# A second down-projection unit moved behind the up unit and the x transposes in the third chunk of each row group

## The chip, the cores and the metric

The kernel runs on one core of one Trainium2 chip. The metric is the device time in microseconds (us); lower is better. Three runs of the kernel before gave a median of 609.52 us (609.05 to 611.1).

The core has a matrix engine (TensorE, PE in the rows), a vector engine (VectorE, DVE), an activation engine (ScalarE, ACT), a general engine (GpSimd, POOL) and a queue that starts transfers (SyncE, SP). Each works through its own list of instructions in order, and they meet at semaphores only.

## The reference, cut to what matters

A feed-forward layer with octonion weights stands beside an autocorrelation term. `x` is 2048 rows of 1024.

```python
xn = layernorm(x)                                  # over the last axis
gate = oct_ternary_linear(xn, w_gate)              # (2048, 2732)
up   = oct_ternary_linear(xn, w_up)                # (2048, 2732)
h    = silu(gate) * up
out  = x + autocorrelation(xn) + oct_ternary_linear(h, w_down)

# oct_ternary_linear: weights rounded to scale * {-1, 0, 1}, then
#   M = einsum('jik,jod->koid', S_OCT, Wq);  einsum('...id,koid->...ko', xp, M)
# autocorrelation(xn): irfft(|rfft(xn)|^2), softmax over the 6 largest lags,
#   the sum of the row rolled by these lags
```

For rows like these lag 0 outweighs all others, so the autocorrelation term is the row itself. The kernel proves this for each row by a bound (a short spectrum and a dot product of the row's two halves) and has a slow path in case it fails.

## The kernel before, in words

**Tiling.** The 2048 rows are 8 groups g of 256. The 2732 hidden values are 3 chunks of 8 x 114. The octonion product is not made by 64 small products: half of it goes through sums and differences of the weights and of the inputs (the spectral part), the other half through single terms. Every result is made of a spectral part in PSUM, eight additions by VectorE over it, and a second series of matmuls on top (the terms).

**Units.** The work is a list of units, `units`. Each takes one of four pairs of PSUM banks in turn, so a unit waits for the last reader of the unit four places ahead of it (`owner`, `take_banks`, `bank_free`). Below, the two digits are chunk and half of the outputs:

- G00 to G21: gate units, 16 matmuls spectral and 16 of terms. Their result goes through silu on ScalarE (`silu`), which frees the banks.
- U00 to U21: up units, of the same size. VectorE multiplies the result by the silu (`product`, in the rows hx by hx and acc), which frees the banks.
- N0 and N1: down units of the group before, one for each 128 rows, 96 matmuls spectral and 96 of terms. VectorE scales them and adds the residual (zx in the rows), which frees the banks.
- X0 and X1: 8 transposes each, of the even and the odd parts of the next group's normalised x. ScalarE and VectorE split them in a high and a low fp16 part and do the same with their sums (`x_high`, `x_low`, `x_sums_high`, `x_sums_low`).
- F: four matmuls of the spectrum for the bound, with four more two places later (`lags`).

At list place n, TensorE issues the spectral part of unit n and then the terms of unit n-2. VectorE does at place n `first_adds` (four, after ScalarE has copied half of the banks by `odd_two`), a due `product` (two places behind its up unit), a due output or `least`, and `second_adds` (four). X units also have `x_low` ahead and the rounding of their sums behind. A product goes to GpSimd, which makes its sums and low parts in six operations; ScalarE makes the high parts (`h_high`, and `h_sums_high` for the sums). At which place ScalarE does these two is set by the tables `high_at` and `round_at`.

**The row statistics.** Two `row_sum` fall at F and at the next G00, two `row_var` one and two places later, the reciprocal root on GpSimd, then two `normalise` on ScalarE and two `dot` on VectorE at N0, for the group whose X units follow.

**Transfers.** The SyncE queue stores the finished rows, reloads zx with the next residual rows, and loads x three groups ahead (`load_x`). All are in one list in order.

## Time and profile before

| | us |
|---|---|
| median of 3 runs | 609.52 (609.05 to 611.1) |
| profiled execution | 609.28 |
| its span, first to last instruction | 607.5 |
| one group in the regular part (start of F to start of F) | 67.33 |
| TensorE busy | 580.5 (96% of the span) |
| VectorE busy | 507.7 (84%) |

The regular part consists of the groups 2 to 6. Group 0 and the weights take the first 90 us, group 7 and the rest the time from 510.55 us on. In a row of the timeline the first number is the start from the span's beginning and the second the duration, both in us; then engine, line, operation, output and inputs, shapes and count. Square brackets at the end name the idle time of that engine just ahead and what ended it. The recorded end of one instruction may lie past the start of the next on the same engine, since they are pipelined: a series of 16 matmuls shows as 1.91 us, and the next starts 1.75 us after its start. A row of a window has its limits and length, then the busy us (and the number of instructions) of PE, PEld, DVE, ACT and POOL, the granted TensorE clock as a share of 2.4 GHz, the share of the DMA engines and GB/s.

### The profile page before, as it was taken

How to read it: one execution, taken by the hardware profiler on the slowest of the kernel's cores; microseconds unless marked ns; L12 is line 12 of the kernel's file. 1: busy time of each engine (PE TensorE's matmuls, PEld its weight loads, DVE VectorE, ACT ScalarE, POOL GpSimd, SP SyncE). 2: the span in 40 equal slices, each digit the busy share in tenths (PEclk: the TensorE clock that was granted, in tenths of full speed). 3: DMA queues.
4: the chain of work that ended last, by engine and by line, in shares of the span. 5: the costliest groups of instructions: out<-in, count | busy, mean ns of one | idle time of the engine just before them, and what ended most of it. 6: DMA issues, size and time to landing. Idle time of an engine off the chain costs nothing.

```text
span 607.5 us, 16365 instructions
## 1 busy us (share of the span) xinstructions
PE 580.5 (96%) x6728; PEld 539.8 (89%) x6728; DVE 507.7 (84%) x1229; ACT 355.4 (59%) x497; POOL 463.0 (76%) x362
## 2 busy tenths in 40 slices
PE   4898999979999999999999999999999999999996
PEld 4898998869989998899989998899989998998896
DVE  3885897969899989989888989989898989967854
ACT  4777867664557646765466545774476545543540
POOL 2404839998769977999769977999779977987920
PEclk9999999998999999999999999999999999999999
DMA  6720012001040012102040013002040112002021
GB/s 163 200 71 1 1 29 113 3 1 70 3 139 1 3 71 87 54 1 71 2 140 2 25 48 136 4 3 71 2 140 1 38 36 71 2 2 71 1 71 72
DMA packets 10235, 30.67 MB, mean 50 GB/s; under 512 B 912, under 2 KB 4016, under 8 KB 10160
## 3 DMA queue, kind: packets, MB, share of 16 engines
q1 hardware_dynamic: 9200, 28.22, 13.8%
q10 hardware_dynamic: 960, 1.40, 1.1%
q8 instruction: 53, 0.87, 0.6%
q14 instruction: 22, 0.18, 0.1%
HBM read 21.23 MB, written 8.39 MB: 49 GB/s over the span
## 4 chain that ended last, share of the span: by engine, by line
POOL 53%; issue 30%; PE 12%; DMA 2%; DVE 1%; ACT 0%; ACTq 0%; POOLq 0%
POOL hop L1320 15%; POOL hs L1314 10%; POOL hs L1315 10%; POOL hs L1310 9%; POOL hs L1309 6%; PE acc L470 5%; PE acc L395 4%; DMA hop<-in_w_gate 2%; PE acc L375 1%; PE acc L447 1%; POOL r L1268 1%; POOL hop L1317 1%; PE acc L404 0%; PE acc L368 0%; ACTq L570 0%
## 5 line engine op out<-in xcount | busy, mean ns | idle before, releaser
L470 PE MATMUL acc<-wd,hop 114*128 114x128 f16 (+1 forms) x2944 | 171.4, 220 | 1.0 <-POOL hop L1320 0.7
L470 PEld LDWEIGHTS acc<-wd,hop 114*128 114x128 f16 (+1 forms) x2944 | 168.3, 98 | 2.2 <-POOL hop L1320 0.9
L679 ACT ACTIVATE pk<-acc 114x512 f32<-114x512 f32 (+1 forms) x120 | 70.8, 590 | 71.7 <-PE acc L470 34.0
L1309 POOL TENSOR_TENSOR hs<-hx 114x512 f32<-114x512 f32 x47 | 60.2, 1282 | 68.3 <-DVE hx L1075 60.3
L1320 POOL TENSOR_TENSOR hop<-hs,hop 114x1024 f16<-114x1024 f32 x46 | 98.2, 2135 | 7.9 <-ACT hop L734 7.9
L1317 POOL TENSOR_TENSOR hop<-hx,hop 114x1024 f16<-114x1024 f32 x46 | 98.3, 2137 | 0.7 <-ACT hop L723 0.7
L375 PE MATMUL acc<-xop,wg 128*128 128x256 f16 x704 | 84.1, 273 | 4.5 <-DVE acc L1026 4.3
L723 ACT ACTIVATE hop<-hx 114x1024 f16<-114x1024 f32 x46 | 48.6, 1057 | 65.4 <-DVE hx L1075 65.4
L368 PE MATMUL acc<-xop,wg 128*128 128x256 f16 x704 | 84.2, 273 | 1.0 <-DVE hx L1075 0.9
L375 PE MATMUL acc<-xop,wu 128*128 128x256 f16 x704 | 84.1, 273 | 0.7
L368 PE MATMUL acc<-xop,wu 128*128 128x256 f16 x704 | 84.1, 273 | 0.7 <-DVE hx L1075 0.7
L978 DVE TENSOR_TENSOR bd<-acc,pk 114x256 f32<-114x256 f32 (+1 forms) x104 | 43.7, 420 | 48.2 <-ACT pk L679 48.1
L375 PEld LDWEIGHTS acc<-xop,wg 128*128 128x128 f16 x704 | 68.3, 98 | 14.2 <-DVE acc L1026 6.0
L368 PEld LDWEIGHTS acc<-xop,wu 128*128 128x128 f16 x704 | 68.7, 98 | 9.1 <-DVE hx L1075 1.0
L368 PEld LDWEIGHTS acc<-xop,wg 128*128 128x128 f16 x704 | 67.7, 98 | 10.2 <-DVE hx L1075 2.6
L375 PEld LDWEIGHTS acc<-xop,wu 128*128 128x128 f16 x704 | 67.8, 98 | 9.9 <-DVE acc L1026 2.4
L734 ACT ACTIVATE hop<-hs 114x1024 f16<-114x1024 f32 x46 | 48.6, 1057 | 45.6 <-POOL hs L1315 45.6
L1314 POOL TENSOR_TENSOR hs<-hs 114x512 f32<-114x512 f32 x47 | 62.4, 1328 | 3.7
L1315 POOL TENSOR_TENSOR hs<-hs 114x512 f32<-114x512 f32 x47 | 62.5, 1331 | 0.0
L1075 DVE SCALAR_TENSOR_TENSOR hx<-hx,few,acc 114x1024 f32<-114x1024 f32 x47 | 59.7, 1271 | 2.1 <-PE acc L395 2.1
L1310 POOL TENSOR_TENSOR hs<-hx 114x512 f32<-114x512 f32 x47 | 60.3, 1282 | 0.0
L982 DVE TENSOR_TENSOR acc<-acc,pk 114x256 f32<-114x256 f32 (+1 forms) x104 | 43.9, 422 | 0.0
(163 smaller groups left out, 922.2 us busy)
## 6 DMA issues: line engine op xcount, KB each, us to landing
xr<-in_x SPq DMA_DIRECT2D x16, 512.0 KB, 5.0
zx<-in_x SPq DMA_DIRECT2D x16, 512.0 KB, 3.9
out_y<-zx SPq DMA_DIRECT2D x16, 512.0 KB, 2.9
hop<-in_w_down SPq DMA_DIRECT2D x1, 1364.0 KB, 6.3
hop<-in_w_gate ACTq DMA_DIRECT2D x1, 1152.0 KB
hop<-in_w_up SPq DMA_DIRECT2D x1, 1152.0 KB
hop<-in_w_gate ACTq DMA_DIRECT2D x1, 192.0 KB
hop<-in_w_up SPq DMA_DIRECT2D x1, 192.0 KB
```

Source lines behind the costliest of these rows:

```text
L368: last = nc.tensor.matmul(acc[:, bank[n], s // 2, T * (s % 2):T * (s % 2 + 1)], wm[:, c, slot, :], xop[:, g % 2, form, level, :], start=s ...
L375: last = nc.tensor.matmul(acc[:, bank[n], s // 2, T * (s % 2):T * (s % 2 + 1)], wm[:, c, slot, :], xop[:, g % 2, form, level, :], start=Fa ...
L470: last = nc.tensor.matmul(acc[:, bank[n], s // 2, at:at + P], operand(g, c, t, form, level), wd[0:WIDE[c], slot, c, :], start=which == 0 a ...
L679: nc.scalar.activation(pk[0:rows, q % 2, :, :], pair[:, :, T:2 * T], ACT.Copy, scale=XS if u[0] == "X" else 1.0).then_inc(copied, 1)
L723: nc.scalar.activation(half_of(g, c, 4 * Y, 0), by_tile(h), ACT.Copy).then_inc(hhi_done, 1)
L1075: nc.vector.scalar_tensor_tensor(hx[0:CH, m % 4, :, :], hx[0:CH, m % 4, :, :], scale[0:CH, :], bank_pair(place[u], CH).rearrange("p b (i t ...
L1309: nc.gpsimd.tensor_tensor(hs[:, 4:8:2, :], h[:, 0:4:2, :], h[:, 1:4:2, :], ALU.add)
L1310: nc.gpsimd.tensor_tensor(hs[:, 5:8:2, :], h[:, 0:4:2, :], h[:, 1:4:2, :], ALU.subtract).then_inc(hpair_done, 1)
L1314: nc.gpsimd.tensor_tensor(hs[:, 0:2, :], hs[:, 4:6, :], hs[:, 6:8, :], ALU.add).then_inc(hs_done, 1)
L1315: nc.gpsimd.tensor_tensor(hs[:, 2:4, :], hs[:, 4:6, :], hs[:, 6:8, :], ALU.subtract).then_inc(hs_done, 1)
L1317: nc.gpsimd.tensor_tensor(half_of(g, c, 4 * Y, 1), by_tile(h), half_of(g, c, 4 * Y, 0), ALU.subtract).then_inc(h_free, 1)
L1320: nc.gpsimd.tensor_tensor(half_of(g, c, NJ + 4 * Y, 1), by_tile(hs[:, 0:4, :]), half_of(g, c, NJ + 4 * Y, 0), ALU.subtract).then_inc(h_rea ...
```

## The change

In groups 1 to 6 the third chunk's list G20, N1, U20, X1, G21, U21 becomes G20, U20, X1, N1, G21, U21. Group 7 has no N1 in that place and stays as it is. With it:

- `round_at` and `high_at` move the roundings of h: behind its unit, U20's high part comes five places later instead of three, U11's high part four instead of three, U10's sums six instead of five.
- The sums of X1 are rounded at the start of the next place (N1's) rather than at its end; VectorE's `x_sums_low` then stands ahead of N1's first additions.
- `normalise` comes after N0's copy on ScalarE, `dot` at the end of N0's place on VectorE; both stood ahead before.
- At the place of U21 the second additions come ahead of N1's output.
- The load of x comes ahead of the second store of a group in SyncE's list, except for the first such load.
- The halves of hop are given out in the order of writing.

Diff:

```diff
--- before.py
+++ after.py
@@ -74,11 +74,13 @@
     for g in range(1, G):
         for c in range(NC):
             units += [("G", g, c, 0)]
-            if c == 1 or c == 2 and g < G - 1:
-                units += [("N", g - 1, c - 1)]
+            if c == 1:
+                units += [("N", g - 1, 0)]
             units += [("U", g, c, 0)]
             if c and g < G - 1:
                 units += [("X", g + 1, c - 1)]
+            if c == 2 and g < G - 1:
+                units += [("N", g - 1, 1)]
             units += [("G", g, c, 1), ("U", g, c, 1)]
             if c == 2 and g < G - 1:
                 units += [("F", g + 1)]
@@ -112,7 +114,11 @@
 
     halves, free_after = {}, {(G - 1, NC - 1): [("U", G - 2, NC - 1, 1)]}
     spare = [(i, None) for i in range(8)]
-    for u in units:
+
+    def written(u):
+        return place[u] + (2.5 if u[0] == "U" and u[2:] == (2, 0) else 0)
+
+    for u in sorted((u for u in units if u[0] in "UN"), key=written):
         if u[0] == "U" and u[3] == 0 and u[1:3] != (G - 1, NC - 1):
             two = sorted(spare[:2])
             spare = spare[2:]
@@ -146,10 +152,12 @@
     for u in u_no:
         _, g, c, Y = u
         if place[u] >= OPEN:
-            late = 6 if g == 0 or c == 2 else 4 if (c, Y, g) == (1, 0, G - 1) else 5
+            inner = 1 <= g < G - 1
+            late = 6 if g == 0 or c == 2 or inner and (c, Y) == (1, 0) else 4 if (c, Y, g) == (1, 0, G - 1) else 5
             if (g, c) == (G - 1, NC - 1):
                 late = 4 + 3 * (1 - Y)
-            high_at[place[u] + 3] = u
+
+            high_at[place[u] + (5 if inner and (c, Y) == (2, 0) else 4 if inner and (c, Y) == (1, 1) else 3)] = u
             round_at[place[u] + late] = u
     for _, g, t in n_no:
         z_at[place["N", g, t] + (t if g == G - 1 else 1 if t == 0 else 2 if g == G - 2 else 3)] = (g, t)
@@ -310,10 +318,12 @@
             for g in range(G):
                 for t in range(NT):
                     k = NT * g + t
+                    if t == 1 and 0 < g and g + 3 < G:
+                        load_x(g + 3)
                     sp.wait_ge(out_done, k + 1)
                     sp.dma_start(out_rows[k, :, :], zx[:, t, :]).then_inc(out_st, 16)
-                    if t == 1 and g + 3 < G:
-                        load_x(g + 3)
+                    if t == 1 and g == 0:
+                        load_x(3)
                     if g < G - 1:
                         sp.wait_ge(out_st, 16 * (k + 1))
                         sp.dma_start(zx[:, t, :], x_rows[k + NT, :, :]).then_inc(zx_in[t], 16)
@@ -797,9 +807,6 @@
             h_high(("U", 0, 1, 0))
 
             for n in range(OPEN, N + 8):
-                if n in norm_at:
-                    normalise(norm_at[n], 0)
-                    normalise(norm_at[n], 1)
                 if n in z_at:
                     g, t = z_at[n]
                     k = NT * g + t
@@ -814,15 +821,20 @@
                     for b in range(2):
                         act.wait_ge(tail_mult, b + 1)
                         nc.scalar.activation(hx[0:CH, LAST % 4, 2 * b + 1, :], last_h[:, 2 * b + 1, :], ACT.Copy).then_inc(tail_odd, 1)
+                if n in x_sums and x_sums[n][2] == 1:
+                    x_sums_high(x_sums[n])
                 if n < N:
                     u = units[n]
                     if u[0] in "GUNX":
                         odd_two(u)
+                    if n in norm_at:
+                        normalise(norm_at[n], 0)
+                        normalise(norm_at[n], 1)
                     if u[0] == "X":
                         x_high(u)
                     if u[0] == "F":
                         power(u)
-                if n in x_sums:
+                if n in x_sums and x_sums[n][2] == 0:
                     x_sums_high(x_sums[n])
                 if n in silu_at:
                     silu(silu_at[n])
@@ -1141,9 +1153,8 @@
                 kind = u[0]
                 if kind == "X":
                     x_low(u)
-                if n in norm_at and kind == "N":
-                    dot(norm_at[n], 0)
-                    dot(norm_at[n], 1)
+                if n in x_sums and x_sums[n][2] == 1:
+                    x_sums_low(x_sums[n])
                 if u in quad_no:
                     first_adds(n, u)
                 if kind == "X":
@@ -1156,25 +1167,31 @@
                         dve.wait_ge(term_mm, prod_no[v] + 1)
                         dve.wait_ge(silu_done, LAST + 1)
                         split_last(v)
-                if n >= OPEN + 2:
-                    v = units[n - 2]
-                    if v[0] == "N":
-                        _, g, t = v
-                        pair = bank_pair(n - 2).rearrange("p b e -> p (b e)")
-                        res = zx[:, t, :]
-                        most = D - DB
-                        dve.wait_ge(term_mm, prod_no[v] + 1)
-                        dve.wait_ge(z_done, n_no[v] + 1)
-                        nc.vector.scalar_tensor_tensor(res[:, 0:most], pair[:, 0:most], osc[:, :], res[:, 0:most], ALU.mult, ALU.add)
-                        nc.vector.scalar_tensor_tensor(res[:, most:D], pair[:, most:D], nosc[:, :], res[:, most:D], ALU.mult, ALU.add).then_inc(out_done, 1)
-                    elif v[0] == "F":
-                        least(v)
-                if u in sums_no:
+                v = units[n - 2] if n >= OPEN + 2 else ("",)
+                if v[0] == "N" and kind == "U":
+
                     second_adds(n, u)
+                if v[0] == "N":
+                    _, g, t = v
+                    pair = bank_pair(n - 2).rearrange("p b e -> p (b e)")
+                    res = zx[:, t, :]
+                    most = D - DB
+                    dve.wait_ge(term_mm, prod_no[v] + 1)
+                    dve.wait_ge(z_done, n_no[v] + 1)
+                    nc.vector.scalar_tensor_tensor(res[:, 0:most], pair[:, 0:most], osc[:, :], res[:, 0:most], ALU.mult, ALU.add)
+                    nc.vector.scalar_tensor_tensor(res[:, most:D], pair[:, most:D], nosc[:, :], res[:, most:D], ALU.mult, ALU.add).then_inc(out_done, 1)
+                elif v[0] == "F":
+                    least(v)
+                if u in sums_no and not (v[0] == "N" and kind == "U"):
+                    second_adds(n, u)
+                if n in norm_at:
+
+                    dot(norm_at[n], 0)
+                    dot(norm_at[n], 1)
                 if kind == "R":
                     dve.wait_ge(flag_mm, 1)
                     nc.vector.tensor_copy(flag[:, :], acc[:, bank[n], 0, 0:1]).then_inc(flag_done, 1)
-                if n in x_sums:
+                if n in x_sums and x_sums[n][2] == 0:
                     x_sums_low(x_sums[n])
                 if n == bound_at:
                     bound()
```

TensorE, third chunk of a regular group, before. In order: spectral part of G20, terms of G11, spectral part of N1, terms of U11, spectral part of U20, terms of G20, X1, terms of N1, spectral part of G21, terms of U20, spectral part of U21, first matmul of F.

```order
L368 MATMUL acc<-xop,wg 128x256 x16
L375 MATMUL acc<-xop,wg 128x256 x16
L470 MATMUL acc<-wd,hop 128x128 x96
L375 MATMUL acc<-xop,wu 128x256 x16
L368 MATMUL acc<-xop,wu 128x256 x16
L375 MATMUL acc<-xop,wg 128x256 x16
L412 MATMUL acc<-ident,xr 128x128 x8
L470 MATMUL acc<-wd,hop 128x128 x96
L368 MATMUL acc<-xop,wg 128x256 x16
L375 MATMUL acc<-xop,wu 128x256 x16
L368 MATMUL acc<-xop,wu 128x256 x16
L425 MATMUL acc<-xop,dft_sb 128x256
```

The same after:

```order
L378 MATMUL acc<-xop,wg 128x256 x16
L385 MATMUL acc<-xop,wg 128x256 x16
L378 MATMUL acc<-xop,wu 128x256 x16
L385 MATMUL acc<-xop,wu 128x256 x16
L422 MATMUL acc<-ident,xr 128x128 x8
L385 MATMUL acc<-xop,wg 128x256 x16
L480 MATMUL acc<-wd,hop 128x128 x96
L385 MATMUL acc<-xop,wu 128x256 x16
L378 MATMUL acc<-xop,wg 128x256 x16
L378 MATMUL acc<-xop,wu 128x256 x16
L480 MATMUL acc<-wd,hop 128x128 x96
L435 MATMUL acc<-xop,dft_sb 128x256
```

Between G20 and N1's spectral part there now stand U20, the terms of U11, X1 and the terms of G20, and N1's terms come just ahead of F.

ScalarE at F and the next G00, before: silu of G21, first row sum, copy of G00, second row sum, its mean, rounding of U20's sums (hop from hs).

```order
L708 ACTIVATE hx<-acc,few 114x1024
L585 ACTIVATE junk,sm<-xr 128x1024
L679 ACTIVATE pk<-acc 114x512
L585 ACTIVATE junk,sm<-xr 128x1024
L588 ACTIVATE nm<-sm 128x2
L734 ACTIVATE hop<-hs 114x2x4x128
```

The same after:

```order
L718 ACTIVATE hx<-acc,few 114x1024
L595 ACTIVATE junk,sm<-xr 128x1024
L744 ACTIVATE hop<-hs 114x2x4x128
L689 ACTIVATE pk<-acc 114x512
L595 ACTIVATE junk,sm<-xr 128x1024
L598 ACTIVATE nm<-sm 128x2
```

The rounding of U20's sums now stands ahead of G00's copy.

SyncE from the store of the second 128 rows of group 0 on (group 1's N1), before. zx from x is a reload of the residual, xr from x a load of x.

```order
L314 DMA out_y<-zx 128x1024
L302 DMA xr<-in_x 128x1024 x2
L319 DMA zx<-in_x 128x1024
L314 DMA out_y<-zx 128x1024
L319 DMA zx<-in_x 128x1024
L314 DMA out_y<-zx 128x1024
L302 DMA xr<-in_x 128x1024 x2
L319 DMA zx<-in_x 128x1024
L314 DMA out_y<-zx 128x1024
```

The same after:

```order
L324 DMA out_y<-zx 128x1024
L310 DMA xr<-in_x 128x1024 x2
L329 DMA zx<-in_x 128x1024
L324 DMA out_y<-zx 128x1024
L329 DMA zx<-in_x 128x1024
L310 DMA xr<-in_x 128x1024 x2
L324 DMA out_y<-zx 128x1024
L329 DMA zx<-in_x 128x1024
L324 DMA out_y<-zx 128x1024
```

The second load of x has moved ahead of the store in front of it; the first one (second row) stays behind its store.

## Rows read from the trace of the kernel before

**Rows 1.** The page, busy time, share of the span and instructions of each engine.

```profile
PE 580.5 (96%) x6728; PEld 539.8 (89%) x6728; DVE 507.7 (84%) x1229; ACT 355.4 (59%) x497; POOL 463.0 (76%) x362
```

**Rows 2.** Timeline of TensorE over one regular group, from F to F.

```profile
241.22 0.28 PE L425 MATMUL acc<-xop,dft_sb 128*128 128x256 f16 x1
...
242.55 1.92 PE L375 MATMUL acc<-xop,wg 128*128 128x256 f16 x16 [0.72 <-DVE acc L1026]
...
249.84 0.60 PE L433 MATMUL acc<-lag_sb,pw 128*128 128x256 f16 x4
...
250.27 1.91 PE L368 MATMUL acc<-xop,wg 128*128 128x256 f16 x16
...
260.75 5.53 PE L470 MATMUL acc<-wd,hop 114*128 114x128 f16 x96
...
271.36 1.04 PE L412 MATMUL acc<-ident,xr 128*128 128x128 f32 x8
...
308.55 0.28 PE L425 MATMUL acc<-xop,dft_sb 128*128 128x256 f16 x1
```

**Rows 3.** Timeline of VectorE over the same group.

```profile
248.51 1.27 DVE L1075 SCALAR_TENSOR_TENSOR hx<-hx,few,acc 114x1024 f32<-114x1024 f32 x1
...
272.36 0.42 DVE L978 TENSOR_TENSOR bd<-acc,pk 114x256 f32<-114x256 f32 x1 [0.27 <-ACT pk L679]
...
280.24 0.42 DVE L978 TENSOR_TENSOR bd<-acc,pk 114x256 f32<-114x256 f32 x1
...
284.09 1.21 DVE L1067 TENSOR_TENSOR xop<-acc,xop 128x1024 f16<-128x1024 f32 x1
...
287.87 0.42 DVE L978 TENSOR_TENSOR bd<-acc,pk 114x256 f32<-114x256 f32 x1
...
292.66 0.42 DVE L978 TENSOR_TENSOR bd<-acc,pk 128x256 f32<-128x256 f32 x1 [2.05 <-ACT pk L679]
...
299.91 1.23 DVE L1058 SCALAR_TENSOR_TENSOR xop<-acc,xop 128x1024 f16<-128x1024 f32 x1 [0.29 <-ACT xop L683]
```

**Rows 4.** Timeline of ScalarE over the same group.

```profile
244.51 1.11 ACT L708 ACTIVATE hx<-acc,few 114x1024 f32<-114x1024 f32 x1 [1.28 <-PE acc L375]
...
246.56 0.58 ACT L679 ACTIVATE pk<-acc 114x512 f32<-114x512 f32 x1
...
248.32 1.04 ACT L734 ACTIVATE hop<-hs 114x1024 f16<-114x1024 f32 x1
...
263.45 2.38 ACT L604 ACTIVATE xr<-xr,nmrs,rs 128x1024 f32<-128x1024 f32 x2 [0.97 <-POOL onep L1279]
...
266.38 0.60 ACT L679 ACTIVATE pk<-acc 128x512 f32<-128x512 f32 x1 [0.55 <-PE acc L470]
...
266.87 1.23 ACT L807 ACTIVATE zx<-zx,nmrs,onep 128x1024 f32<-128x1024 f32 x1
...
305.75 1.02 ACT L688 ACTIVATE xop<-acc 128x1024 f16<-128x1024 f32 x1
```

**Rows 5.** One source line, the dot products: duration ns min/median/max, first and last start.

```profile
L937 DVE SCALAR_TENSOR_TENSOR dj<-xr x16: 683/694/1571, 31.4 to 468.7; 128x512 f16<-128x512 f32 x16
```

**Rows 6.** Output of N1 on VectorE, SyncE's load of x, and its landing (us).

```profile
170.42 0.34 DVE L1169 SCALAR_TENSOR_TENSOR zx<-acc,few,zx 128x128 f32<-128x128 f32 x1
...
171.24 1.20 SPq L302 DMA_DIRECT2D xr<-in_x  x2
...
DMA to landing us min/median/max: 4.8/5.3/5.7
```

**Rows 7.** Group 1: TensorE and VectorE, and the window that gives the granted clock.

```profile
134.59 1.09 PE L412 MATMUL acc<-ident,xr 128*128 128x128 f32 x8 [2.76 <-DVE hx L1075]
...
135.93 7.16 PE L470 MATMUL acc<-wd,hop 114*128 114x128 f16 x96 [0.25 <-DVE acc L1000]
...
136.00:138.00 2.00, 2.00 (x23) 2.00 (x24) 1.85 (x6) 2.00 (x5) 2.00 (x2) 0.58 0.00 0
...
136.15 0.42 DVE L978 TENSOR_TENSOR bd<-acc,pk 114x256 f32<-114x256 f32 x1 [0.27 <-ACT pk L679]
```

## The prediction

> **What bounds the kernel now.** I read the busy shares first: TensorE is busy for 96% of the span and VectorE for 84% [rows 1], so little can be won, and VectorE is close behind. Then TensorE's timeline over a regular group, from F at 241.22 to the next F at 308.55, 67.33 us [rows 2]. Its own work, from starts to starts: 24 series of 16 matmuls at 1.747 (six of them fill 250.27 to 260.75) are 41.9; four halves of down units at 5.37 (the recorded 5.53 less the 0.16 by which a recorded end overlaps the next start) are 21.5; two X at 0.87 (1.04 less the same) are 1.7; F and lags at 0.43 each (249.84 to 250.27) are 0.9 [rows 2]. Sum 66.0. So 1.3 us a group are waits, 0.72 of them flagged at the terms of G21, which wait for VectorE's second additions [rows 2]. Between the spectral part of G21 and its terms lie only two series and F, 3.9 us.
>
> Then VectorE. From U10's first additions (272.36) to N1's (292.66) it stands still only once, 2.05 us ahead of N1, where it waits for the copy [rows 3]. That pause is what the old order has as a reserve: TensorE is 5.4 us at N1's spectral part while VectorE finishes G20.
>
> **The change part by part.** Times below are from the start of F (241.22 is 0).
>
> *TensorE's order.* G21 and U21 get N1's 5.4 us of terms between their two halves, so the 0.72 and the small waits behind it go. Worth up to 1.3 a group. Against it, U20, X1, N1 now follow each other without N1's matmuls between G20 and U20.
>
> *F to N0.* Silu of G21 starts at 3.29 [rows 4]; the terms of G21 now start 0.87 earlier (at 0.46 for 1.33), so 2.42. Then 1.01 for silu, 1.04 for the row sum (244.51 to 246.56 less silu) and, new ahead of G00's copy, the rounding of U20's sums, 0.97 (1.04 less overlap) [rows 4]: the copy starts at 5.44 where the bare order would have 4.5, ends at 6.02. VectorE's additions cost 0.33 each (280.24 to 287.87 is 16 additions, a product of 1.19 and a rounding of 1.13, both less the 0.08 of overlap) [rows 3]; four more and the product of U21 (1.27) [rows 3] end at 8.65. G01 needs U21's banks and starts at 8.70, where the bare matmuls would be there at 7.88: a new wait of 0.8. From there six series: N0's spectral part at 19.18 (now 260.75, 19.53) [rows 2], its end 24.71. Won so far: 0.35 of 1.3.
>
> *N0.* ScalarE: copy at 24.78 (0.1 behind as now, 266.38), 0.49; two normalise 2.28; residual 1.13 [rows 4]; two roundings of h at 0.97; copy of U10 0.58. End 31.19, so VectorE can start U10 at 31.22. VectorE: N0's four additions from 25.39, product 1.19, four additions, to 29.24, then the dots. In the rows a dot takes 0.69 or 1.57 [rows 5]; with both and the reads of the accumulator 2.3, so 31.55, with two short ones 30.7. U10's first additions start at 31.2 to 31.55 (now 31.14) [rows 3]. Moving dots and normalise thus wins nothing ahead of U10: N0's additions come sooner, but the same work stands in the same chain.
>
> The long dot is where it meets GpSimd: the Trainium skill ("GPSIMD Engine Reference", Key points) says that GpSimd shares SBUF interfaces with VectorE instructions of two SBUF inputs, which a dot is. By that rule the late dots still meet GpSimd's low part of U00's sums, and the start is 31.55; without it 31.2. The trace has both lengths, and I take the middle.
>
> *From U10 to F.* Now VectorE works without a break, D being the start of U10: to G11 7.88 (272.36 to 280.24), to G20 7.63 more (280.24 to 287.87), G20 itself 2.65: D+18.16 [rows 3]. Then new: U20's eight additions and U11's product 3.85 (280.24 to 284.09 is the same content) to D+22.0. U11's banks are what N1's spectral part waits for: D+20.8. X1: 1.13 and nine additions, 4.12 (from the 1.23 row and 0.33 each) [rows 3], to D+26.1. Then VectorE waits for ScalarE's rounding of X1's sums, 1.02 and two hand-overs [rows 4]: it goes on at D+27.3 with 1.13 (x_sums_low, 1.21 less overlap) [rows 3], N1's four additions, U20's product: D+31.03. U21's spectral part needs U20's banks: D+31.1. Then TensorE 1.75 for it, 5.37 for N1's terms, and F at D+38.2. With D = 31.2 to 31.55 a group takes 69.4 to 69.75, middle 69.6. TensorE waits in it at G01 (0.8), at N1's spectral part (0.7 to 0.8), at U21 (about 1.4) and in crumbs; 66.0 plus these makes the same sum. Against 67.33 that is +2.3. GpSimd (76%) [rows 1] I charge nothing: U20 and U21 reach it 14 us apart now. If that fails, it shows as N0's matmuls waiting for hop.
>
> *Group 1.* Today X0 waits 2.76 and the clock drops to 0.58 behind it, so N0's terms take 7.16 for 5.53 [rows 7]. Both go, since the product of U01 no longer stands behind the dots. But normalise starts when GpSimd's root is there, as now, and VectorE's U10 starts at about 135.0 for 136.15 [rows 7]: 1.15 earlier. From there to F it is 37.7 now (F at 241.22 less 67.33, so 173.9) and 38.2 after: 0.5 back. Net -0.7 of the 4.4 that it seems to promise.
>
> *Load of x.* From the second load on it goes out when X1's transposes are done, some 20 us ahead of its row sum. The first stays behind the store, and N1's output now comes just behind F: it ends at 1.6. Today the load is issued 0.48 behind that output's end (170.76, 171.24) and the first half lands 4.8 later [rows 6]: 6.9. The row sum wants it at 3.4. So group 2 starts with 3.5 more ahead of the rounding, G00's copy, U21's product and G01, and TensorE idles 4.3 there. In group 1 an idle time of 2.76 cost 1.63 more in clock, at the 0.58 of a stretch that is mostly at 1.2 GHz [rows 7]; none or all of that may follow here, I take 1.0. Sum for group 2: 2.3 + 3.5 + 1.0 = +6.8.
>
> *Group 7* starts as the others (0.35 won ahead of N0) and has neither X nor dots: -0.35.
>
> **Sum.** Group 1 -0.7, group 2 +6.8, groups 3 to 6 4 x 2.3 = +9.2, group 7 -0.35: +14.9. On the profiled 609.3 (span 607.5 and 1.8 around it, 0.2 under the median) that is 624.2. Ends from the bounds: groups at 69.4, no clock loss, 622; at 69.75 and the full loss, 625.5.
>
> **Rivals.**
>
> *The aim is met (faster).* VectorE keeps up, the 1.3 go in five groups (-6.5) and 4.4 in group 1: 598.5, or 602 with the late load. For it: the flagged wait sits just where the change gives room. Against: VectorE's unbroken stretch [rows 3] has lost its pause. It decides at N1's spectral part: if that starts under 50.5 from F, this holds. Chance 0.08.
>
> *Roughly even.* One link of the chain D to F is not there, for instance X1's rounding done before VectorE arrives, or U20's banks free earlier, which takes 1.2 to 2.3 a group off: 609 to 617. Chance 0.12.
>
> *Load in time.* The transfer alone lands sooner or the row sum is not in front of the copy: the chain stays, without 4.5: 619.7. Chance 0.12.
>
> *Clock.* The 1.4 us wait at U21 drops the clock in each group as the 2.76 did: 1.6 x 5 more, 632. Waits of 0.72 show no such loss in the regular groups, whose series stay at 1.91 [rows 2]. No row has a wait of 1.4. The Trainium skill ("TensorE: Matmul & The Clock Gate", Part 1) has TensorE drop from 2.4 to 1.2 GHz when it has idled; applied to every wait at U21 it gives the 632, applied to the gap of 4.3 alone the forecast. Chance 0.08.
>
> *Forecast* as summed: 0.60.
>
> **How the numbers follow.** Predicted 624. A difference of 0.3% (1.8 us) is about what can be told from none here. Faster: the first rival and the lower tip of nothing else, 0.08. Same: a third of the even one, 0.05. Slower: 0.87. The range from 614 to 630 leaves out the first rival, a third of the second and most of the clock case.
>
> **What would show it.** F to F 69.4 to 69.75 in groups 3 to 6; U10's first additions 31.2 to 31.55 from F; TensorE waits at G01 on VectorE's product, at N1's spectral part and at U21's, each on a product; VectorE idle 1.2 ahead of x_sums_low of X1; the flagged 0.72 gone; group 1 without its 2.76; a wait of ScalarE for a DMA of x of 3.5 once, at F of group 2. Wrong if N1's spectral part starts before 51 from F, or F to F is under 67.3.

## The result, and the profile after

The changed kernel took 631.5 us (median of six, 630.49 to 631.93) against 609.29 for the kernel before in the same comparison: 3.7% slower, ratio 1.0366 (95% interval 1.0339 to 1.0393). The forecast was slower, at 624 with a range of 614 to 630. The profiled execution has a span of 628.7 us, 21.2 more than before.

TensorE over one regular group after, timeline, from F to F:

```profile
250.50 0.28 PE L435 MATMUL acc<-xop,dft_sb 128*128 128x256 f16 x1
...
259.16 1.92 PE L378 MATMUL acc<-xop,wg 128*128 128x256 f16 x16 [0.64 <-DVE hx L1087]
...
269.78 5.53 PE L480 MATMUL acc<-wd,hop 114*128 114x128 f16 x96
...
290.94 1.92 PE L378 MATMUL acc<-xop,wu 128*128 128x256 f16 x16 [0.65 <-DVE zx L1182]
...
293.44 1.92 PE L378 MATMUL acc<-xop,wg 128*128 128x256 f16 x16 [0.59 <-DVE hx L1087]
...
303.72 5.54 PE L480 MATMUL acc<-wd,hop 114*128 114x128 f16 x96 [0.49 <-DVE hx L1087]
...
313.99 1.92 PE L378 MATMUL acc<-xop,wu 128*128 128x256 f16 x16 [1.25 <-DVE hx L1087]
...
321.11 0.27 PE L435 MATMUL acc<-xop,dft_sb 128*128 128x256 f16 x1
```

These rows answer to [rows 2]. The start of F to the start of F is 70.61 for 67.33. The flagged wait of the terms of G21 is gone. In its place stand waits for VectorE: at G01 (259.16), G20 (293.44), at N1's spectral part (303.72) and at U21's (313.99) for a product (L1087), and at U11 (290.94) for the output of N0 (L1182). N0's spectral part starts 19.28 from F (before 19.53).

VectorE in the same group, timeline:

```profile
276.04 0.42 DVE L990 TENSOR_TENSOR bd<-acc,pk 128x256 f32<-128x256 f32 x1 [2.46 <-ACT pk L689]
...
279.89 0.68 DVE L949 SCALAR_TENSOR_TENSOR dj<-xr 128x512 f16<-128x512 f32 x1
...
280.68 2.43 DVE L949 SCALAR_TENSOR_TENSOR dj<-xr 128x512 f16<-128x512 f32 x1
...
283.05 0.08 DVE L949 DVE_READ_ACCUMULATOR dj<-xr 128x1 f32 x1
...
290.80 0.41 DVE L990 TENSOR_TENSOR bd<-acc,pk 114x256 f32<-114x256 f32 x1
...
298.42 0.41 DVE L990 TENSOR_TENSOR bd<-acc,pk 114x256 f32<-114x256 f32 x1
...
310.20 1.22 DVE L1079 TENSOR_TENSOR xop<-acc,xop 128x1024 f16<-128x1024 f32 x1 [1.09 <-ACT xop L698]
```

They answer to [rows 3]. U10's first additions (283.05) start 32.55 from F, before 31.14. The second dot takes 2.43 us, before 1.57. From there VectorE has no idle time until the 1.09 ahead of X1's sums (310.20); the 2.05 ahead of N1 is gone.

ScalarE in the same group, timeline, for [rows 4]:

```profile
254.94 1.04 ACT L744 ACTIVATE hop<-hs 114x1024 f16<-114x1024 f32 x1
...
255.88 0.58 ACT L689 ACTIVATE pk<-acc 114x512 f32<-114x512 f32 x1
...
275.41 0.60 ACT L689 ACTIVATE pk<-acc 128x512 f32<-128x512 f32 x1 [3.61 <-PE acc L480]
...
275.90 2.36 ACT L614 ACTIVATE xr<-xr,nmrs,rs 128x1024 f32<-128x1024 f32 x2
...
309.14 1.02 ACT L698 ACTIVATE xop<-acc 128x1024 f16<-128x1024 f32 x1 [3.67 <-DVE acc L1022]
```

The rounding of U20's sums stands ahead of G00's copy (254.94, 255.88). Normalise starts right behind N0's copy, and ScalarE waits 3.67 for the sums of X1 (309.14).

All groups, as starts of F in the span (us), and what lies between:

| | F of group 1 | group 1 | group 2 | groups 3 to 6, each | last F to the end |
|---|---|---|---|---|---|
| before | 100.33 | 73.55 | 67.34 | 67.33 | 96.95 |
| after | 100.40 | 73.97 | 76.13 | 70.61 | 95.74 |
| difference | +0.1 | +0.4 | +8.8 | 4 x +3.28 | -1.2 |

"Group g" runs here from the F in front of it to the next one. The sum is +21.2, the difference of the spans.

In group 1 X0's wait of 2.76 is gone, but TensorE waits 1.59 at U11 (143.22) and 1.56 at G20 (146.70) instead.

### The profile page after: what moved, and what is told of

Read it like the earlier page. It is cut to its first block, busy times and chain, and to the rows that moved or that the text cites. A ratio compares the mean times of both kernels' runs of the same rounds, so it can differ in the third digit from the quotient of the medians.

```text
span 628.7 us, 16365 instructions
## 1 busy us (share of the span) xinstructions
PE 582.8 (93%) x6728; PEld 538.4 (86%) x6728; DVE 511.5 (81%) x1229; ACT 354.4 (56%) x497; POOL 461.7 (73%) x362
## 4 chain that ended last, share of the span: by engine, by line
POOL 54%; issue 30%; PE 12%; DMA 2%; DVE 1%; ACT 0%; ACTq 0%; POOLq 0%
POOL hop L1337 15%; POOL hs L1331 9%; POOL hs L1327 9%; POOL hs L1332 9%; POOL hs L1326 7%; PE acc L480 5%; PE acc L405 4%; POOL hop L1334 3%; DMA hop<-in_w_gate 2%; PE acc L385 1%; PE acc L457 1%; POOL r L1285 1%; PE acc L414 0%; PE acc L378 0%; ACTq L580 0%
## 5 line engine op out<-in xcount | busy, mean ns | idle before, releaser
L480 PEld LDWEIGHTS acc<-wd,hop 114*128 114x128 f16 (+1 forms) x2944 | 166.4, 98 | 6.4 <-DVE hx L1087 4.6
L1334 POOL TENSOR_TENSOR hop<-hx,hop 114x1024 f16<-114x1024 f32 x46 | 98.6, 2144 | 21.2 <-ACT hop L733 21.2
L1326 POOL TENSOR_TENSOR hs<-hx 114x512 f32<-114x512 f32 x47 | 62.4, 1328 | 43.5 <-DVE hx L1087 36.2
L385 PEld LDWEIGHTS acc<-xop,wg 128*128 128x128 f16 x704 | 69.1, 98 | 8.6 <-issue 0.4
L385 PEld LDWEIGHTS acc<-xop,wu 128*128 128x128 f16 x704 | 68.3, 98 | 7.7
L744 ACT ACTIVATE hop<-hs 114x1024 f16<-114x1024 f32 x46 | 48.4, 1053 | 38.3 <-POOL hs L1332 38.1
L1331 POOL TENSOR_TENSOR hs<-hs 114x512 f32<-114x512 f32 x47 | 59.7, 1270 | 3.7
L1087 DVE SCALAR_TENSOR_TENSOR hx<-hx,few,acc 114x1024 f32<-114x1024 f32 x47 | 59.7, 1270 | 2.1 <-PE acc L405 2.1
L1327 POOL TENSOR_TENSOR hs<-hx 114x512 f32<-114x512 f32 x47 | 60.3, 1283 | 0.0
L1332 POOL TENSOR_TENSOR hs<-hs 114x512 f32<-114x512 f32 x47 | 59.8, 1272 | 0.0
```

The costliest lines, as they stand in the source:

```text
L385: last = nc.tensor.matmul(acc[:, bank[n], s // 2, T * (s % 2):T * (s % 2 + 1)], wm[:, c, slot, :], xop[:, g % 2, form, level, :], start=Fa ...
L480: last = nc.tensor.matmul(acc[:, bank[n], s // 2, at:at + P], operand(g, c, t, form, level), wd[0:WIDE[c], slot, c, :], start=which == 0 a ...
L1087: nc.vector.scalar_tensor_tensor(hx[0:CH, m % 4, :, :], hx[0:CH, m % 4, :, :], scale[0:CH, :], bank_pair(place[u], CH).rearrange("p b (i t ...
L1326: nc.gpsimd.tensor_tensor(hs[:, 4:8:2, :], h[:, 0:4:2, :], h[:, 1:4:2, :], ALU.add)
L1327: nc.gpsimd.tensor_tensor(hs[:, 5:8:2, :], h[:, 0:4:2, :], h[:, 1:4:2, :], ALU.subtract).then_inc(hpair_done, 1)
L1331: nc.gpsimd.tensor_tensor(hs[:, 0:2, :], hs[:, 4:6, :], hs[:, 6:8, :], ALU.add).then_inc(hs_done, 1)
```

## The experiments

Each is an edit of the changed kernel ("after") or of the one before ("before"), run beside the kernel before. F to F is read from the starts of F in its trace, and the argument rests on it rather than on the medians: F of group 1 comes between 99.0 and 102.3 us in these traces, and the four runs of round_u20_later alone lie between 623.25 and 628.03 (see the last section).

| kernel | median us | ratio to before (95%) | group 1 | group 2 | groups 3 to 6 |
|---|---|---|---|---|---|
| before | 609.29 | | 73.55 | 67.34 | 67.33 |
| after | 631.5 | 1.0366 (1.0339 to 1.0393) | 73.97 | 76.13 | 70.61 |
| short_dots | 625.05 | 1.0267 (1.0231 to 1.0303) | 73.07 | 74.68 | 69.37 |
| first_load | 625.29 | 1.0281 (1.0240 to 1.0322) | 73.98 | 70.61 | 70.62 |
| early_dots | 625.42 | 1.0261 (1.0229 to 1.0294) | 73.96 | 75.17 | 69.1 to 69.3 |
| round_u00_later | 636.91 (one run) | | 73.98 | 78.01 | 71.6 |
| x_sums_back | 624.55 | 1.0270 (1.0228 to 1.0313) | 72.62 | 76.45 | 69.27 |
| round_u20_later | 627.32 | 1.0285 (1.0233 to 1.0336) | 74.03 | 75.38 | 69.68 |
| before_late_dots | 614.73 | 1.0098 (1.0062 to 1.0134) | 71.96 | 68.85 | 68.85 |
| old_order | 630.3 | 1.0368 (1.0318 to 1.0417) | 73.53 | 71.04 | 71.04, one 72.70 |
| combo_b | 606.43 | 0.9963 (0.9943 to 0.9983) | 74.24 | 67.08 | 67.07 |
| combo_c | 606.36 | 0.9949 (0.9927 to 0.9971) | 72.64 | 67.10 | 67.10 |

**short_dots**: what the dots cost where they stand. From group 2 on the kernel leaves out all but 8 of the 512 pairs of each dot product.

```diff
-                nc.vector.scalar_tensor_tensor(dj[:, :], xr[:, t, 0:D // 2], 1.0, xr[:, t, D // 2:D], ALU.mult, ALU.mult,
+                part = D // 2 if g < 2 else 8
+                nc.vector.scalar_tensor_tensor(dj[:, 0:part], xr[:, t, 0:part], 1.0, xr[:, t, D // 2:D // 2 + part], ALU.mult, ALU.mult,
```

> From group 2 on each dot product covers 8 of its 512 pairs, so the bound that guards the lag-0 shortcut is not the true one there; all else is the changed kernel. Theory (the second dot, 2.43 us beside GpSimd's low part, delays the start of U10, and everything up to the next F hangs on it): U10 starts on VectorE when ScalarE's copy of it is there, 31.3 us from F for 32.55, F to F falls from 70.6 to 69.4, and the run by about 1.25 x 6 = 7.5, to 624. Rival (ScalarE's row of normalise, residual and roundings sets the pace, the dot only fills its time): F to F stays 70.6, 631.5.

U10 starts 31.30 from F for the expected 31.3, F to F is 69.37 for 69.4, the run takes 625.05. The rival falls: the dot was on the path by 1.24 us a group.

The two dots that fall in group 1 show more, since GpSimd is at work there. The second one, with 8 pairs, and the GpSimd operation beside it, timeline:

```profile
132.16 1.98 DVE L950 SCALAR_TENSOR_TENSOR dj<-xr 128x8 f16<-128x8 f32 x1
```

```profile
131.99 2.13 POOL L1335 TENSOR_TENSOR hop<-hx,hop 114x1024 f16<-114x1024 f32 x1
```

An instruction of 0.17 us elsewhere takes 1.98 and ends at 134.14, 0.02 behind the end of GpSimd's.

**round_u00_later**: is it GpSimd that makes the dot long?

```diff
+            if (c, Y) == (0, 0) and 1 <= g < G - 1:
+                late = 6
             round_at[place[u] + late] = u
```

> The changed kernel with ScalarE's rounding of U00's sums one place later, so that GpSimd has no low part to make while the dots run. Theory (the dot waits for the GpSimd operation in progress): both dots take 0.7 us. Rival (the second dot is long by itself, or by ScalarE's work on zx beside it): 2.4 stays. For the time this is no gain: U10 starts 1.6 earlier, but GpSimd gets to U01 some 3 us later, ScalarE waits for its sums ahead of G11's copy, and F to F comes out between 70.5 and 72.5.

VectorE and GpSimd in this kernel, timeline around the dots of a regular group:

```profile
353.98 0.68 DVE L951 SCALAR_TENSOR_TENSOR dj<-xr 128x512 f16<-128x512 f32 x1
...
354.77 0.69 DVE L951 SCALAR_TENSOR_TENSOR dj<-xr 128x512 f16<-128x512 f32 x1
```

```profile
357.09 2.13 POOL L1339 TENSOR_TENSOR hop<-hs,hop 114x1024 f16<-114x1024 f32 x1 [4.33 <-ACT hop L746]
```

With GpSimd idle both dots take 0.7 us. This is one run, and its time is used for nothing else. Now the rows with a long dot, timeline of the same two engines, before:

```profile
266.66 1.57 DVE L937 SCALAR_TENSOR_TENSOR dj<-xr 128x512 f16<-128x512 f32 x1
```

```profile
265.95 1.73 POOL L1314 TENSOR_TENSOR hs<-hs 114x512 f32<-114x512 f32 x1
```

and GpSimd after (the dot that it meets is the one at 280.68 above):

```profile
280.42 2.15 POOL L1337 TENSOR_TENSOR hop<-hs,hop 114x1024 f16<-114x1024 f32 x1 [1.77 <-ACT hop L744]
...
282.53 1.72 POOL L1326 TENSOR_TENSOR hs<-hx 114x512 f32<-114x512 f32 x1
```

Both long dots end 0.54 to 0.55 us behind the end of the GpSimd operation that was under way (before 268.23 and 267.68; after 283.11 and 282.57), and the GpSimd operation that comes up while a dot runs is longer: 1.72 to 1.73 for the 1.27 of the same operation elsewhere. So the dot waits for GpSimd's operation and then needs 0.55; it doesn't run slowly beside it, which the 8 pairs of short_dots settle: had GpSimd only slowed them, 0.17 us of work would not have ended with its operation, both times. F to F is 71.6, in the expected 70.5 to 72.5.

The Trainium skill says this outright in "SBUF — State Buffer" ("Who interferes with whom"): the shared pair of ports is an exclusive lock, held for the whole instruction by whichever engine came first, and a VectorE instruction with two SBUF inputs contends with a GpSimd one that reads SBUF. The rows agree: each engine's instruction stands until the other's is over. I had weighed the line that names the shared interfaces and not this one, from which the size follows: the rest of the GpSimd operation in progress.

**first_load**: why group 2 is 5.5 us longer than its successors.

```diff
-                    if t == 1 and 0 < g and g + 3 < G:
+                    if t == 1 and g + 3 < G:
                         load_x(g + 3)
                     sp.wait_ge(out_done, k + 1)
                     sp.dma_start(out_rows[k, :, :], zx[:, t, :]).then_inc(out_st, 16)
-                    if t == 1 and g == 0:
-                        load_x(3)
```

> The changed kernel with the first load of x too ahead of its store. Theory (the row sum at F of group 2 waits 3.9 us for it, and TensorE's 4.6 us of idling behind it lowers its clock): the wait on the DMA goes, the G00/G01 series of group 2 run at full clock, and group 2 gets as long as the others, 76.1 to 70.6: 626.0. Without the clock's part it would be only 3.9 less, 627.6. Rival (group 2 is longer since the opening's backlog on GpSimd ends there): nothing changes, 631.5.

Timeline rows of ScalarE and TensorE after, at the start of group 2, and its windows (limits, length, busy time and count of PE, weight loads, DVE, ACT and POOL, then the granted clock, the DMA share and GB/s):

```profile
181.73 1.06 ACT L595 ACTIVATE junk<-xr 128x1024 f16<-128x1024 f32 x1 [3.87 <-DMA xr<-in_x]
```

```profile
187.01 3.02 PE L378 MATMUL acc<-xop,wg 128*128 128x256 f16 x16 [4.62 <-DVE hx L1087]
```

```profile
184.00:186.00 2.00, 0.00 (x0) 0.00 (x0) 1.66 (x5) 1.55 (x4) 2.00 (x1) 1.00 0.07 27
...
186.00:188.00 2.00, 0.99 (x8) 0.85 (x9) 2.00 (x5) 1.02 (x2) 1.00 (x2) 0.91 0.00 0
...
188.00:190.00 2.00, 2.00 (x11) 1.42 (x10) 1.73 (x6) 1.65 (x4) 1.92 (x3) 0.50 0.00 0
```

The row sum waits 3.87 for the load; TensorE idles 4.62, its G01 series then takes 3.02 for 1.92, and the clock of the window 188 to 190 is 0.50, the lower level of 1.2 GHz. In first_load the same windows read:

```profile
184.00:186.00 2.00, 2.00 (x21) 1.80 (x19) 1.73 (x6) 1.89 (x4) 1.92 (x3) 1.00 0.00 0
...
186.00:188.00 2.00, 2.00 (x19) 1.60 (x18) 2.00 (x7) 1.54 (x3) 2.00 (x3) 1.00 0.00 0
...
188.00:190.00 2.00, 2.00 (x21) 1.79 (x20) 2.00 (x7) 2.00 (x4) 1.95 (x1) 1.00 0.00 0
```

Group 2 takes 70.61, exactly as the others, 5.5 less; the median is 625.29 for the expected 626.0. 3.97 of the 5.5 stand ahead of G01 (12.64 from F for 8.67); the 1.55 that are left come with the stretch at the lower clock.

**early_dots**: normalise and dots back in front of N0 (three lines of `normalise` moved from behind `odd_two` to the start of the place, three of `dot` from the end of the place to ahead of `first_adds`).

```diff
             for n in range(OPEN, N + 8):
+                if n in norm_at:
+                    normalise(norm_at[n], 0)
+                    normalise(norm_at[n], 1)
                 if n in z_at:
...
+                if n in norm_at and kind == "N":
+                    dot(norm_at[n], 0)
+                    dot(norm_at[n], 1)
                 if u in quad_no:
                     first_adds(n, u)
```

> The changed kernel with normalise and the dots ahead of N0's copy and additions again; order of units, roundings and loads as changed. Theory (the late place puts both in VectorE's and ScalarE's unbroken stretch, the early one uses the idle time ahead of N0's copy, 2.5 us on VectorE and 3.6 on ScalarE): U10 starts at about 30.2 from F for 32.55, F to F 68.3, in group 1 nothing won since normalise waits for GpSimd's root there; 631.5 less 5 x 2.3 = 620. Rival (the dots just wait for normalise and push N0 as far as they came forward): F to F 70.6 or more, 631.

VectorE's timeline in group 3 (F at 251.05) and group 5 (F at 389.70):

```profile
274.63 1.80 DVE L949 SCALAR_TENSOR_TENSOR dj<-xr 128x512 f16<-128x512 f32 x1 [0.51 <-ACT xr L614]
...
276.54 1.57 DVE L949 SCALAR_TENSOR_TENSOR dj<-xr 128x512 f16<-128x512 f32 x1
...
282.25 0.42 DVE L990 TENSOR_TENSOR bd<-acc,pk 114x256 f32<-114x256 f32 x1 [0.27 <-ACT pk L689]
...
419.78 0.42 DVE L990 TENSOR_TENSOR bd<-acc,pk 114x256 f32<-114x256 f32 x1 [0.27 <-ACT pk L689]
...
428.46 0.42 DVE L990 TENSOR_TENSOR bd<-acc,pk 114x256 f32<-114x256 f32 x1 [0.79 <-ACT pk L689]
```

The direction holds, the size does not: F to F is 69.1 to 69.3, not 68.3. In groups 3 and 4 the early place meets GpSimd too: both dots are long (1.80 and 1.57), U10 starts 31.20 from F, 1.35 sooner than in the changed kernel, and F to F is 69.3, 1.3 less. In groups 5 and 6 one dot is short and U10 starts at 30.1 as expected, 2.5 sooner, but F to F is 69.1, only 1.5 less. There VectorE waits 0.79 for G11's copy, since TensorE's own G11 comes no sooner.

**x_sums_back**: X1's sums rounded at the end of N1's place.

```diff
-                if n in x_sums and x_sums[n][2] == 0:
+                if n in x_sums:
                     x_sums_high(x_sums[n])
...
-                if n in x_sums and x_sums[n][2] == 0:
+                if n in x_sums:
                     x_sums_low(x_sums[n])
```

(with the two lines each for `== 1` at the start of the place removed)

> The changed kernel with the rounding of X1's sums at the end of N1's place again (ScalarE's part behind N1's copy, VectorE's behind N1's second additions). Theory (ScalarE's 1.0 and VectorE's 1.1 stand in the chain from U10 to F): N1's additions start when its copy is there, 1.4 earlier, TensorE's 1.25 of waiting at U21's spectral part goes, F to F 70.6 to 69.3, the run to 631.5 less 6 x 1.3 = 623.7. Rival (the next F or G00 needs X1's sums early, so the wait moves there): 70.6 or longer.

69.27 for the expected 69.3, and the wait at U21 is not in the trace any more.

**round_u20_later**: U20's rounding behind G00's copy.

```diff
+            if inner and (c, Y) == (2, 0):
+                late = 7
```

> The changed kernel with the rounding of U20's sums behind G00's copy and the second row sum (late = 7 for it). Theory (this rounding delays G00's copy by 0.94 and by it U21's product, for which G01's banks wait 0.64): that wait goes and F to F falls by 0.64 to 70.0, the run by 3.8 to 627.7. Rival (GpSimd, which now waits longer for the rounding, gets U21 to N0 too late, or the copy was free): no gain, or matmuls of N0 waiting for hop.

69.68: 0.94 less, the full time of the rounding, where 0.64 was expected. The wait at G01 is gone, and the crumb behind it too. N0 does not wait for hop.

**before_late_dots**: the two late moves alone, in the kernel before.

```diff
                     if u[0] in "GUNX":
                         odd_two(u)
+                    if n in norm_at:
+                        normalise(norm_at[n], 0)
+                        normalise(norm_at[n], 1)
...
                 if u in sums_no:
                     second_adds(n, u)
+                if n in norm_at:
+                    dot(norm_at[n], 0)
+                    dot(norm_at[n], 1)
```

> The kernel before with normalise and the dots late, nothing else. Theory: the late dots collide with GpSimd there too (2.4 us), U10 starts at about 32.5 from F for 31.1, and TensorE waits 0.5 to 0.9 for N0's output and G11's additions in a regular group, while VectorE's 2.05 ahead of N1 shrink: F to F 67.8 to 68.3; group 1 loses its 2.76 wait and the slow clock, 2.7 less. In all 609 to 611. Rival (the late dots are harmless where VectorE has its pause): F to F 67.33 and 606.5.

TensorE's and VectorE's timeline in a regular group:

```profile
271.25 0.68 DVE L937 SCALAR_TENSOR_TENSOR dj<-xr 128x512 f16<-128x512 f32 x1
...
272.04 2.43 DVE L937 SCALAR_TENSOR_TENSOR dj<-xr 128x512 f16<-128x512 f32 x1
```

```profile
282.29 1.92 PE L368 MATMUL acc<-xop,wu 128*128 128x256 f16 x16 [0.65 <-DVE zx L1166]
...
284.81 1.92 PE L368 MATMUL acc<-xop,wg 128*128 128x256 f16 x16 [0.59 <-DVE hx L1075]
```

```profile
294.56 0.42 DVE L978 TENSOR_TENSOR bd<-acc,pk 128x256 f32<-128x256 f32 x1 [2.05 <-ACT pk L679]
```

The long dot is the same 2.43, and TensorE waits for N0's output (0.65), as expected, and for U10's product ahead of G20 (0.59), where I had expected G11's additions. 68.85 a group is 1.52 more than before and more than the 0.5 to 1.0 expected: the run is at 614.73, above both forecasts. VectorE's pause ahead of N1 lies behind these two waits and doesn't take them back; it is 2.05 as before (294.56).

**old_order**: the changed kernel with the old list of units.

```diff
-            if c == 1:
-                units += [("N", g - 1, 0)]
+            if c == 1 or c == 2 and g < G - 1:
+                units += [("N", g - 1, c - 1)]
             units += [("U", g, c, 0)]
             if c and g < G - 1:
                 units += [("X", g + 1, c - 1)]
-            if c == 2 and g < G - 1:
-                units += [("N", g - 1, 1)]
```

> The changed kernel with the list of units as before (N1 right behind G20), all else as changed. Theory (the late dots cost 1.5 in any order, the new order of the third chunk with X1's early rounding and the late N1 the rest, and the late first load hurts only where N1's output comes behind F): F to F 68.9 to 69.4, group 2 as long as the others, about 617. Rival (the moved roundings and dots are the whole loss): 629 to 632.

The theory falls but for one part: group 2 is as long as the others, so the late first load costs nothing where N1's output comes early. The time is the rival's number, 630.3, but that match is partly chance, since it holds two drops of TensorE's clock of about 1.7 us each, which come in some groups and not in others. The run doesn't isolate the order either. With the old list U11's high part, four places behind its unit, lands ahead of X1's copy, and TensorE's F now waits 1.43 for U20's product. TensorE's timeline in the one group that took 72.70, and behind the last F:

```profile
314.87 0.28 PE L433 MATMUL acc<-xop,dft_sb 128*128 128x256 f16 x1 [1.43 <-DVE hx L1085]
...
316.20 3.58 PE L383 MATMUL acc<-xop,wg 128*128 128x256 f16 x16 [0.72 <-DVE acc L1036]
...
387.57 0.28 PE L433 MATMUL acc<-xop,dft_sb 128*128 128x256 f16 x1 [1.43 <-DVE hx L1085]
...
530.99 3.37 PE L383 MATMUL acc<-xop,wg 128*128 128x256 f16 x16 [0.73 <-DVE acc L1036]
```

**combo_b**: early_dots, x_sums_back, round_u20_later and first_load together; what is left of the change is the order of units, the order of writing, and the places of the other roundings.

> The changed order of units with four steps undone or added: dots and normalise early, X1's sums late, U20's rounding one later, the first load ahead too. Theory (each is a link of its own in one chain, or frees the next): of the waits of a group only 0.5 at N1's spectral part and crumbs are left, F to F 67.2, group 1 about 72, and the run about 605, 4 under the kernel before. Rival (VectorE's work in a row from G11 on sets the pace in any case, links overlap): F to F 68 to 69, 612 to 617.

VectorE's and TensorE's timeline in a regular group:

```profile
297.62 0.42 DVE L988 TENSOR_TENSOR bd<-acc,pk 128x256 f32<-128x256 f32 x1 [0.87 <-ACT pk L689]
```

```profile
240.35 0.27 PE L435 MATMUL acc<-xop,dft_sb 128*128 128x256 f16 x1
...
291.36 5.54 PE L480 MATMUL acc<-wd,hop 114*128 114x128 f16 x96 [0.49 <-DVE hx L1085]
...
307.41 0.28 PE L435 MATMUL acc<-xop,dft_sb 128*128 128x256 f16 x1
```

67.07 for the expected 67.2. Of TensorE's waits over 0.3 us only the 0.49 at N1's spectral part is left, and VectorE has 0.87 of idle time ahead of N1's additions. 606.43 is 0.4% under the kernel before (interval 0.2 to 0.6%). It is 1.4 over the expected 605: group 1 is at 74.24 for about 72, since it keeps X0's wait of 2.76.

**combo_c**: in combo_b, normalise and dots late in group 1 alone.

```diff
-                if n in norm_at:
+                if n in norm_at and norm_at[n] > 2:
                     normalise(norm_at[n], 0)
                     normalise(norm_at[n], 1)
...
+                    if norm_at.get(n) == 2:
+                        normalise(2, 0)
+                        normalise(2, 1)
...
+                if norm_at.get(n) == 2:
+                    dot(2, 0)
+                    dot(2, 1)
```

> combo_b with normalise and dots late in group 1 alone, where GpSimd's root comes late anyway. Theory: there the late place wins, since the product of U01 no longer stands behind the dots and X0 does not wait 2.8 us with the slow clock behind it; group 1 gets as long as in x_sums_back, 72.6 for 74.2, and the run 1.6 shorter, 604.8. Rival (the collision of the dots with GpSimd, 1.6 and 2.4 us, eats that): 606.4.

Group 1 takes 72.64, as expected 1.6 less. The time doesn't follow: 606.36 for 604.8 expected, which is the rival's number. The profiled spans are both 604.4, because combo_c's F of group 1 came at 100.52 and combo_b's at 99.03: what the first stretch with its weight transfers takes differs by that much between executions. Against its own runs of before it is at 0.9949, against 0.9963; the intervals overlap, so that combo_c is the faster is shown by the group, not by the time.

## Why the prediction was wrong

The sign held, and so did the chain with TensorE's waits at the places named. The sum was 6 us short (+14.9 for the +21.2 of the spans; another 1 us lies between the median and the profiled execution). By its own steps:

**TensorE's order.** Right: the flagged wait went. Three waits came, at the three places named; two smaller ones, for N0's output and for U10's product, were hidden in "crumbs" and are there because U10 started a microsecond late (in short_dots the first is gone and the second at 0.18).

**F to N0.** Forecast G01 at 8.70 and N0's spectral part at 19.18; measured 8.66 and 19.28. round_u20_later shows the rounding as the cause of the wait at G01.

**N0, the dots: the step that failed.** I took the ends for a dot from [rows 5], 0.69 and 1.57, so 2.3 at most for both with their reads, put U10's start at 31.2 to 31.55 and chose the middle. The two took 3.16 (279.89 to 283.05), and U10 started at 32.55. 1.57 was no end: it was what a dot costs that meets a GpSimd operation of 1.27 us under way, and I had myself placed GpSimd's low part, which takes 2.13, beside the moved dot. The right term was what remains of the other engine's operation plus 0.55, as round_u00_later, short_dots and the pairs of rows show. I had written that the engines meet at semaphores only, and the sum charged GpSimd nothing and looked for its trouble at N0's matmuls; here GpSimd held up a VectorE instruction that uses nothing its own operation makes. The miss is 1.0 in each of five groups.

**Group 1.** Forecast -0.7, measured +0.4, 1.1 more. U10 started at 135.33 for 135.0, with both dots long (1.62 and 2.43), and from there to F it was 39.0 for 38.2. The dots hold GpSimd up as well: its two operations beside them take 2.58 and 2.59 for 2.13, and ScalarE's rounding waits for the sums that GpSimd makes behind them, and the copy of G11 for the rounding, for which VectorE waits 0.88 (144.04). In short_dots these two operations take 2.13 each, and group 1 is 0.9 shorter.

**From U10 to F.** Forecast 38.2, measured 38.06, link by link: G11 at 7.75 for 7.88, N1's spectral part at 20.67 for 20.8, U21's at 30.94 for 31.1. x_sums_back confirms the link at U21. early_dots shows how far the chain holds: with U10 at 31.20 F comes 38.1 behind it, with U10 at 30.1 it comes 39.0 behind, held by G11's copy.

**Load of x.** The 3.5 was 3.97 ahead of G01, and where I had taken 1.0 for the clock it was 1.55. Together 1.0 too little, which first_load shows.

**Group 7.** -1.2 for -0.35. I had let it start as the others, with the wait at G01. But ScalarE has no row sum there: G00's copy comes 4.34 from F for 5.38, G01 starts without a wait at 7.86, and N0's spectral part at 18.35 for 19.54 before. By luck this error hides 0.85 of the others.

**What I said of the cause.** I put the loss down to the order of units having taken VectorE's pause. The experiments don't bear that out: the late dots cost 1.52 a group in the old order, pause and all, and 1.3 to 1.5 in the new one; and with dots, X1's sums and U20's rounding put back the new order has 67.07, 0.26 under before. Of 70.61 to 67.07, x_sums_back gives 1.34, round_u20_later 0.94 and early_dots 1.3 to 1.5 when undone one at a time, 3.6 to 3.8 of 3.54 in all. So the regular groups' loss is in the moves that go with the new order, not in the order. What the order alone brings, with nothing fitted to it, stays open: the only run with the old list had tables that don't fit it.

## What to carry to other kernels

Where two engines can hold each other up, bound the cost of a moved instruction by the other engine's operation at the new place, not by the longest of its own durations so far. When a list of work is reordered, check each small instruction that was moved along with it for what queues behind it on its own engine; here three of them, each 0.9 to 1.5 us, cost 3.5 where the reorder with them undone gives 0.26. A chain link that goes saves only down to the next chain: early_dots took 1.35 out in two groups and won 1.3, and 2.5 in two others and won 1.5.

## What the runs showed of the hardware

A VectorE instruction with two SBUF inputs of 512 fp32 elements (0.69 us alone) ended 0.55 us after the GpSimd tensor_tensor that was running, whether that was one of 1.27 or of 2.13 us, and took 1.57 to 2.43 in all. A GpSimd operation that came up behind a dot took 1.72 for 1.27, or 2.58 for 2.13. A dot of 8 pairs took 0.15 to 0.17 with GpSimd idle, and 1.10 and 1.98 where a GpSimd operation was under way, ending 0.02 to 0.03 behind it.

TensorE's waits of 1.25 us left its clock at the higher level in every regular group after (granted clock 1.00 from 312 to 318). In old_order a wait of 1.43 at F and one of 0.72 behind it come six times. Four times the clock stays and the series behind takes 1.92. Twice it falls to the lower level: at 316.20 the series takes 3.58, with a granted clock of 0.56 and 0.59 in the two windows from 316 to 320, and the group 72.70 for 71.04; at 530.99 it takes 3.37, with 0.57 and 0.58 from 531 to 535. So a pair of waits that is harmless in one group cost 1.66 us in another of the same kernel.

The same shows between executions. In all twelve traces TensorE waits 1.98 or 1.99 us at about 52 us, well ahead of group 1. In nine the way from the first F to the second takes 55.25; in early_dots, round_u00_later and round_u20_later it takes 56.9, and in early_dots the granted clock is 0.50 from 54 to 56, where it is 1.00 after. What decides it these runs don't show.
